# Handing out the transfers of the negated maxima from ScalarE's queue, an earlier split of the first cross maxima, and two more cross tiles bounded by VectorE

## What is computed

```
x = x + attn(layernorm(x))                       # causal, rope, 16 heads over 4
x = x + xattn(layernorm(x), ctx, ctx, mask)      # 16 heads, softmax over 256 keys
x = x + ffn(layernorm(x))                        # relu, hq = float_quantize(h, 4, 3), @ float_quantize(w2).T
```

## Time and profile before

| | |
|---|---|
| median of 3 runs | 1726.19 us (1725.86 to 1730.09) |
| profiled execution | 1726.77 us, of which the span on the core 1725.1 us |
| granted TensorE clock, mean over the span | 0.982 |
| PE (TensorE) busy | 1617.5 us, 94% |
| DVE (VectorE) busy | 1159.0 us, 67% |
| ACT (ScalarE) busy | 1116.1 us, 65% |
| POOL (GpSimd) busy | 753.5 us, 44% |

### The profile page before, as it was taken

The page is one execution under the profiler, slowest core; times in us unless marked ns, Lnnn a source line. Parts: engine busy times, 40 slices in busy tenths (PEclk is TensorE's granted clock), DMA queues, the critical chain, the costliest instruction groups (busy, mean ns, idle before and its releaser), DMA issues.

```text
span 1725.1 us, 33722 instructions
## 1 busy us (share of the span) xinstructions
PE 1617.5 (94%) x11950; PEld 973.6 (56%) x11950; DVE 1159.0 (67%) x1736; ACT 1116.1 (65%) x1733; POOL 753.5 (44%) x1010
## 2 busy tenths in 40 slices
PE   3879999999999999999999999999999999999988
PEld 2445556656555565655656555665655556565555
DVE  4557576685857758586676858668585775857573
ACT  4455675766668566665856567576666856666574
POOL 2252344644345553444545334464434555344410
PEclk7979999999999999999999999999999999999999
DMA  7473453754547374553845546375454737454420
GB/s 182 59 99 70 68 85 65 103 95 64 96 60 107 68 96 90 75 84 57 119 72 81 94 66 89 65 103 95 64 96 60 106 68 96 90 75 73 62 40 13
DMA packets 106238, 140.17 MB, mean 81 GB/s; under 512 B 12385, under 2 KB 74242, under 8 KB 105954
## 3 DMA queue, kind: packets, MB, share of 16 engines
q1 hardware_dynamic: 103090, 130.96, 51.0%
q0 software_dynamic: 2352, 8.26, 1.5%
q10 hardware_dynamic: 768, 0.57, 0.1%
HBM read 21.29 MB, written 8.39 MB: 17 GB/s over the span
## 4 chain that ended last, share of the span: by engine, by line
PE 75%; DMA 9%; ACT 6%; DVE 4%; issue 3%; POOL 2%; SPq 1%; DVEq 0%; ACTq 0%; POOLq 0%
PE o_pair L1457 14%; PE score L1418 8%; PE small L1543 7%; DMA Q<-negT 5%; PE small L1577 5%; PE o_pair L1288 5%; PE small L1288 4%; PE score L1395 3%; PE small L1304 3%; PE score L1341 3%; DVE negmax L1021 2%; PE score L1376 2%; PE small L1470 2%; DMA sums<-o_sb 2%; PE score L1400 2%
## 5 line engine op out<-in xcount | busy, mean ns | idle before, releaser
L1021 DVE TENSOR_REDUCE negmax<-score 128x4 f32<-128x1024 f32 (+1 forms) x384 | 456.9, 1216 | 73.4 <-PE score L1376 47.0
L780 ACT ACTIVATE P<-score 128x1024 f32<-128x1024 f32 x448 | 446.4, 1026 | 74.6 <-PE score L1418 26.4
L1053 DVE TENSOR_TENSOR P<-P,cross_bound 128x1024 f32<-128x1024 f32 x192 | 230.8, 1250 | 88.6 <-ACT P L780 88.5
L1457 PE MATMUL o_pair<-P,V 128*32 128x256 f32 (+1 forms) x4096 | 280.0, 362 | 2.6 <-DVE P L1053 2.4
L828 ACT ACTIVATE score<-cross_q 128x1024 f32<-128x1024 bf16 x192 | 196.3, 1023 | 46.4 <-DVE negmax L1021 42.9
L1418 PE MATMUL score<-Q,K 99*128 99x256 bf16 x1024 | 152.3, 276 | 25.9 <-DMA Q<-negT 24.8
L1457 PEld LDWEIGHTS o_pair<-P,V 128*32 128x32 f32 x4096 | 87.8, 108 | 134.6 <-issue 73.4
L1577 PE MATMUL small<-xnT,w 128*128 128x256 f32 x600 | 157.6, 381 | 0.0
L1418 PEld LDWEIGHTS score<-Q,K 99*128 99x128 bf16 x1024 | 83.7, 98 | 125.7 <-ACT P L780 61.7
L558 POOL TENSOR_TENSOR x<-x,ffn 128x1024 f32<-128x1024 f32 x15 | 32.8, 2189 | 268.9 <-DVE negmax L1021 268.9
L1376 PE MATMUL score<-K,Q 96*128 96x256 bf16 x768 | 121.0, 282 | 9.9 <-ACT score L828 5.4
(11 more groups left out here) (202 smaller groups left out, 3049.4 us busy)
## 6 DMA issues: line engine op xcount, KB each, us to landing
K<-k2p SPq DMA_DIRECT2D x96, 256.0 KB, 6.2
Q<-q2p SPq DMA_DIRECT2D x192, 128.0 KB, 5.2
Q<-q1p SPq DMA_DIRECT2D x90, 256.0 KB, 6.7
x_in<-in_x SPq DMA_DIRECT2D x16, 512.0 KB, 5.3
ctxT<-in_ctx SPq DMA_DIRECT2D x16, 512.0 KB, 7.1
k2f<-q1f SPq DMA_DIRECT2D x32, 256.0 KB, 6.3
inT<-o_sb SPq DMA_DIRECT2D x60, 128.0 KB
o<-inverse SPq DMA_DIRECT2D x60, 128.0 KB
```

The costliest lines, as they stand in the source:

```text
L780: A.activation(P[:, t % 4, :], score[b][:, :, :], ACT.Exp, scale=SCALE).then_inc(score_free[b], 1)
L1021: V.tensor_reduce(negmax[:, k, h:h + 1024 // w], s.rearrange("p (h w) -> p h w", w=w), AX.X, ALU.max, negate=True).then_inc(score_free[b], 1)
L1053: V.tensor_tensor(p, p, cross_bound[:, t % 2, :].unsqueeze(1).broadcast_to([128, 4, SEQ]), ALU.min).then_inc(probs_masked[1], 1)
L1457: last = T.matmul(o_ps[ob][32 * j:32 * j + 32, SEQ * gg + q0:SEQ * gg + SEQ], v, p, start=s == 0, stop=end, tile_position=(0, 32 * j), ski ...
```

## The change

1. The four transfers of negated maxima per group move from SyncE's queue (`put_neg`, removed) to ScalarE's: `maxima` waits for its own copy and hands out the transfer itself.
2. In the first cross pass `cut_first(1, i, 0)` goes before `premask(10)`, `cut_second` from tile 11 to right behind `premask(10)`, and `maxima(st, 1, 0)` from behind `premask(13)` to behind tile 12. On GpSimd `cut_rest` and `cut_third` of (cross, 0) go ahead of the rope sum of k1 and of the first part of q1.
3. Cross tiles 7 and 11 of the second pass are bounded by VectorE too: only 3 and 15 keep TensorE's mask.
4. VectorE's statistics of the next group's input go out of the cross bounds to behind the twelve self row maxima, and GpSimd's inverse root of them from before `keys_rest` to before the bound of self tile 3.

```diff
-        BOUNDED = (N1 - 2, 3 * UNITS)
+        MASK_ADDED = (3, N2 - 1)
+        BOUNDED = (N1 - 2, N2 - len(MASK_ADDED))
...
-            u, s = t // TPU[a], t % TPU[a]
-            if a == 0:
-                return t - (t > 2) if t not in (2, N1 - 1) else None
-            return 3 * u + s if s < 3 else None
+            added = (2, N1 - 1) if a == 0 else MASK_ADDED
+            return t - sum(m < t for m in added) if t not in added else None
...
-            def put_neg(st, a, b):
-
-                name, at = f"m{a + 1}T_{b}", slice(SEQ * b, SEQ * b + SEQ)
-                sp.wait_ge(small_free[st.bank(name)], st.this(name))
-                to = Q1[KROWS:SROWS, :, at] if a == 0 else Q2[KROWS:SROWS, b]
-                sp.dma_start(to, negT[a][:, at]).then_inc(neg_stacked[a][b], 16)
...
@@ gpsimd body
-                if nxt:
-                    inverse_root(0, i + 1)
...
                 for t in range(N1):
+                    if nxt and t == 3:
+                        inverse_root(0, i + 1)
...
+                cut_rest(1, i, 0)
+                if nxt:
                     rope_sum("k1", k1s, i + 1)
+                cut_third(1, i, 0)
+                if nxt:
                     part("q1", 0, whole, part1, i + 1)
-                cut_rest(1, i, 0)
-                cut_third(1, i, 0)
-                if nxt:
                     rest("q1", i + 1)
...
@@ scalar maxima
                 A.activation(negT[a][:, at], bank[:, :].bitcast(bf16)[0:3 * HEADS, 0:SEQ], ACT.Copy).then_inc(free, 1)
+                act.wait_ge(free, st.this(name))
+                to = Q1[KROWS:SROWS, :, at] if a == 0 else Q2[KROWS:SROWS, b]
+                act.dma_start(to, negT[a][:, at]).then_inc(neg_stacked[a][b], 16)
...
@@ scalar body
                 for t in range(3, N2):
+                    if t == 10:
+                        cut_first(1, i, 0)
                     if t not in PE_MASKED:
                         premask(i, t)
                     if prev and t in EVICT_AFTER:
                         hidden(st, [3 + EVICT_AFTER.index(t)])
                     if t == 10:
-                        cut_first(1, i, 0)
-                    if t == 11:
                         cut_second(1, i, 0)
-                    if t == 13:
+                    if t == 12:
                         maxima(st, 1, 0)
...
@@ vector cross_bounds and body
-                    if t == 11 and nxt:
-                        dve.wait_ge(x_loaded, 16 * (i + 2))
-                        block_stats(0, x_in, range(3))
-                if nxt:
-                    norm_stats(0, x_in, i + 1, range(3, NBLK))
...
-                    if not prev and t == 8:
-                        dve.wait_ge(x_loaded, 16 * (i + 2))
-                        norm_stats(0, x_in, i + 1)
+                if nxt:
+                    dve.wait_ge(x_loaded, 16 * (i + 2))
+                    norm_stats(0, x_in, i + 1)
                 if prev:
```

More of the change, by code:

```diff
@@ L436, in body @@
                 if prev:
-                    put_neg(st, 1, 1)
                     put_part("q1", 2, i)
@@ L447, in body @@
                     put_inverses2(i - 1)
-                put_neg(st, 0, 0)
                 put_part("k2", 0, i)
-                put_neg(st, 0, 1)
                 for n in range(1, 3):
@@ L460, in body @@
                     sp.dma_start(ctxT[:, :, :], ctx_v[i + 1]).then_inc(ctx_loaded, 16)
+                if nxt:
                     put_part("q1", 0, i + 1)
-                put_neg(st, 1, 0)
-                if nxt:
                     put_part("k1", 0, i + 1)
@@ L471, in _ @@
             body(NG - 1, True, False)
-            put_neg(END, 1, 1)
             for r in range(2):
@@ L646, in body @@
                     rope_products("k1", cosk, sink, k1s, i + 1)
+                cut_rest(1, i, 0)
+                if nxt:
                     rope_sum("k1", k1s, i + 1)
-                    part("q1", 0, whole, part1, i + 1)
-                cut_rest(1, i, 0)
                 cut_third(1, i, 0)
                 if nxt:
+                    part("q1", 0, whole, part1, i + 1)
                     rest("q1", i + 1)
@@ L1164, in _, with cross_bounds @@
             V.tensor_tensor(q1p[:, 2, :, SEQ:TOK], q[1], q1p[:, 1, :, SEQ:TOK], ALU.subtract).then_inc(part3["q1"], 1)
-            def cross_bounds(st, g, i=None, nxt=False):
+            def cross_bounds(st, g, i=None):
                 for t in range(N2):
@@ L1183, in body @@
                 if prev:
-                    cross_bounds(st, i - 1, i, nxt)
+                    cross_bounds(st, i - 1, i)
                 for t in range(N1):
```

## The result

The changed kernel takes 1863.08 us (median of 4, 1858.97 to 1868.75), beside 1728.14 for the kernel before in the same session: ratio 1.078, 95% interval 1.0764 to 1.0799. It was forecast at 1717 and is 135 us slower than before. The profiled execution took 1858.97 us, at a mean granted clock of 0.956; the profiled one of before had 0.982.

The account below looks back on a forecast made before the run. TensorE, busy 94%, was taken as the bound. Handover -0.87, second cross pass -0.30 and self pass +0.46, 15 times, gave -10.7; end part and sixteenth self pass +1.6; together -9.1, so 1717 us, range 1703 to 1729.

Parts of the forecast that it names:

- the part on the rest: Remaining effects, among them SyncE's queue losing four issues: what was stuck behind them is not waited for; counted as nothing.
- The handover term: From body to body: earlier negT transfer closes TensorE's 1.61 us wait, tile 13 held 0.74; -0.87 a body, 15 times.
- my rival of the landing: DMA engines, not the issue, bind the landing: handover stays, ScalarE's other two issues still cost; 1730 us, chance 0.13.
- The issue time: X, ScalarE's time to issue one negT transfer: taken as 0.78 us, ends 0.44 and 0.85.
- the tiles it holds: ScalarE's issue delays TensorE: 0.74 us at tile 13, 0.56 at cross exponential 4, 0.46 at self exponential 2.
- The rival of a ScalarE held for 1.2 us: Own-copy wait plus issue holds ScalarE 1.2 us, paid at three places on TensorE's path: +11, 1737 us, chance 0.08.
- The masks: Second cross pass: two masks off TensorE save 0.86 us a body, VectorE's two added bounds staying hidden.
- The statistics: Input statistics moved before VectorE's self-pass residual: counted as nothing, with 0 and 0.3 us as ends.
- The end part: After the last body: no handover wait to close, so +0.74 us once, and +0.4 for the two added bounds.

Follow-up runs that it names:

- run 7: Changed kernel with SyncE holding K2 until the self maxima landed, and K1, later query parts and the next input until the cross maxima landed: 1796.44 us.
- run 2: Changed kernel with the four transfers of negated maxima back on SyncE's queue in their old places, all else as changed: 1736.83 us.
- run 3: Kernel before with only the two more bounded cross tiles and the moved input statistics and inverse root; cut and issue unchanged: 1722.13 us.
- run 9: Kernel before with only SyncE's order altered, to that in which large and small transfers start in the changed kernel: 1919.6 us.
- run 1: Kernel before with only the four transfers of negated maxima moved from SyncE's queue to ScalarE's: 1839.06 us.
- run 4: Changed kernel with SyncE holding K2's later parts, k1, the second query part and the next input, but not K2's first part: 1874.91 us.
- run 12: Kernel before with run 3's edits; on SyncE's queue, first cross transfer ahead of q1's parts, second q1 and k1 parts behind the second: 1713.55 us.

## Why the prediction was wrong

**The step that failed** is the last sentence of the part on the rest: SyncE's queue loses four issues, and "what was stuck behind them (last parts of q1 and k1, the next input) is not waited for". It asked only who waits for the released transfers. It did not ask whom they would now overtake, and its list leaves out K2, which the two self transfers had held back. Their release is a term of the sum, and I had set it at 0: it measured 1.95 + 2.25 + 1.63 = 5.8 us of waits in the body shown, 79.4 us over the kernel, and the slower clock after them.

**The handover term** failed as well: -1.61 was booked because "with the same 6.09 us it lands at 643.77". A landing time is no property of a transfer. It took 7.89 us, since its end is tied to q1's first part, about 10 us after that is given out; the wait stayed at 1.63. This is what my rival of the landing had said, at a chance of 0.13, and run 7 bears it out. Its price of 1730 was still short by 133, since it too took the other three transfers to be free: it saw large transfers that already stood ahead, and not those that the change would put there. The earlier cut, which was to help this term, delays q1's first part and costs 14.7 us by itself with SyncE's issue (run 2 against run 3).

**The issue time** was right: 0.72 us, priced at 0.78. So were the tiles it holds: 0.66 at tile 13 (priced 0.74), 0.60 at exponential 4 (0.56) and 0.56 at exponential 2 (0.46). The rival of a ScalarE held for 1.2 us falls with it.

**The masks** were right where they stand: 0.86 a body. But of it 0.35 arrived (run 3), for the reason in the next paragraph. In the loop VectorE kept up with the two added bounds.

**The statistics** did cost. Their delay of the residual had 0 and 0.3 us as ends and was counted as nothing; it measured about 0.2 a body (run 3), and the 0.34 of GpSimd's bound came with them and the inverse root. In the change itself the longer waits for the maxima hide both. That in another order most of 72 us would hang on where they stand could not be read from their own rows.

What stays open is the size: the runs show that a small transfer lands 0.6 to 1.6 us behind the last large one given out before it, where that one lands late, and three distances from the issue of the first (10 us for q1's three, 8.8 for K2's first two, of which the second was still being given out, 13.2 for K2's three in run 9), but no rule that gives them for another mix. The end part was not tried by itself. Nor was the earlier cut with ScalarE's issue, so of the 24 us between run 1 and the change only the 14.7 of run 2 and the masks' 7 the other way are known from runs.

## What to carry to other kernels

A wait on a queue also holds back what is queued behind it. Before moving a small, urgent transfer to another queue, list the large ones that its wait was holding, and ask which of them will start ahead of it; here another queue gave no way past them. Read a landing from the issue and the landing of what stands ahead, and when two kernels are compared check that this distance is the constant one. Check too, in the profile of an experiment, that a wait which was added does hold what it should: that of run 4 did not. If the order is then mended, every small transfer of the chain must be followed: what is pushed behind the first is put ahead of the second.

## What was not expected of the hardware

- A transfer of 24 KB landed 9.96 to 10.00 us after the issue of the three 256 KB transfers ahead of it, in the bodies shown, whether it was itself given out 2.1 or 3.9 us after them, on the same queue or on another; with nothing large behind it, 9.44. With nothing large ahead that had not landed, such a transfer took 2.7 to 3.2 us.
- ScalarE's issue of it took 0.72 us (median of 64), SyncE's 0.78; one partition of it 0.61.
- The added waits cost twice. The matmuls of the changed kernel were busy 40.0 us longer than the same ones of run 12, at a mean clock of 0.956 against 0.981.
